# ScalarE's functions regrouped by activation table in a Mamba and mixture-of-experts kernel

## The reference, cut to what matters

```python
xn = layernorm(x)
x = x + filter_block(xn) + moe_by_sequence(xn)   # L0
xn = layernorm(x)
x = x + causal_attention(xn) + moe_by_token(xn)  # L1, 16 heads; 2 of 8 experts per token

# filter_block (L0_attn), cut:
u    = silu(conv(u_in) + conv_b)                 # 256 channels, 4 taps
dt, B, C = split(u @ x_proj)
delta = softplus(dt @ dt_proj + dt_b)
h[t] = exp(delta[t]*A) * h[t-1] + delta[t]*B[t]*u[t]   # 16 states, a scan over t
m    = ((h . C) + u*D_skip) * silu(res) @ out_proj
h    = layernorm(m + x)
q = gelu(l2norm(h @ q_w + q_b));  k = l2norm(h @ k_w + k_b)
qw = q . w_g;  G = (l2norm_over_tokens(qw) * q).sum(tokens)
hs = (G * k) @ proj + proj_b
hs = (hs * layernorm(h)) @ fl + fl_b
h2 = layernorm(hs + h)
out = layernorm(gelu(h2 @ d1 + d1_b) @ d2 + d2_b + h2)

# moe_by_sequence (L0_ffn): softmax router on the mean of the sequence, its best 2 of 8
# experts (gelu between two matmuls), weighted sum, + x, layernorm
```

## Time and profile before

| | us |
|---|---|
| median of 3 runs | 2735.15 |
| lowest, highest | 2718.67, 2745.57 |
| the profiled execution, its own time | 2738.27 |
| its span | 2736.5 |

### The profile page before, as it was taken

One profiled execution on the slowest core, in us unless ns is written; L12 is line 12 of the kernel. 1 busy time (PEld: TensorE's weight loads), 2 busy tenths in 40 slices (PEclk: granted clock), 3 DMA queues, 4 the chain that ended last, 5 costly groups with the idle time before them and its releaser, 6 DMA issues.

```text
span 2736.5 us, 38788 instructions
## 1 busy us (share of the span) xinstructions
PE 2185.6 (80%) x11640; PEld 1519.0 (56%) x11640; DVE 1644.7 (60%) x2929; ACT 1177.2 (43%) x2702; POOL 936.8 (34%) x581
## 2 busy tenths in 40 slices
PE   4257888888888788888889788987889788888885
PEld 1033566655665556655566556655666555665664
DVE  2965775557754776547764587546765477644322
ACT  2223454345533455345543465333553345423541
POOL 0421562028410473006620185103740067202501
PEclk8568889888999889989899898898899988999997
DMA  2000011311222111321113112221113211131123
GB/s 94 0 16 0 32 50 62 113 51 46 68 82 75 53 41 58 106 76 41 51 64 104 61 46 70 70 88 50 44 59 97 85 37 56 59 126 58 62 93 115
DMA packets 82452, 175.06 MB, mean 64 GB/s; under 512 B 11448, under 2 KB 42560, under 8 KB 81984
## 3 DMA queue, kind: packets, MB, share of 16 engines
q1 hardware_dynamic: 78144, 164.05, 17.9%
q0 software_dynamic: 4096, 8.40, 1.1%
HBM read 123.71 MB, written 15.14 MB: 51 GB/s over the span
## 4 chain that ended last, share of the span: by engine, by line
PE 49%; issue 17%; DVE 15%; POOL 9%; ACT 7%; DMA 1%; SPq 0%; DVEq 0%; POOLq 0%; ACTq 0%
PE G L910 8%; PE G L1032 6%; DVE HS L1509 3%; PE G L1017 3%; POOL Y L1925 3%; PE G L921 2%; PE FM L1006 2%; POOL REG L1936 2%; PE G L1049 2%; PE FM L731 2%; POOL YG L1950 2%; DVE maxes L1803 2%; PE G L1006 2%; POOL REG L1939 2%; PE FM L880 2%
## 5 line engine op out<-in xcount | busy, mean ns | idle before, releaser
L1032 PEld LDWEIGHTS G<-REG 128*128 128x128 f32 x2560 | 376.8, 213 | 79.2 <-issue 53.6
L1032 PE MATMUL G<-REG 128*128 128x64 f32 x2560 | 383.7, 286 | 18.9 <-DVE REG L1815 18.9
L1312 ACT ACTIVATE REG<-G 128x128 f32<-128x128 f32 (+3 forms) x512 | 224.1, 438 | 374.9 <-PE G L1017 371.5
L1509 DVE TENSOR_TENSOR_SCAN HS<-DA,D 128x1024 f32<-128x1024 f32 x128 | 361.8, 2827 | 31.3 <-ACT DA L1191 30.7
L1925 POOL TENSOR_TENSOR Y<-Y,HC 128x1024 f32<-128x1024 f32 x114 | 274.8, 2410 | 258.0 <-DVE HC L1531 257.4
L910 PEld LDWEIGHTS G<-XGT,MW 128*128 128x128 f32 x1920 | 294.9, 238 | 58.1 <-issue 58.1
L910 PE MATMUL G<-XGT,MW 128*128 128x128 f32 x1920 | 301.9, 324 | 19.5 <-DMA MW<-moe 19.5
L1936 POOL TENSOR_TENSOR REG<-REG,cos_t 128x512 f32<-128x512 f32 x128 | 170.4, 1331 | 341.8 <-ACT REG L1288 340.7
L1017 PE MATMUL G<-ident,REG 128*128 128x128 f32 x1280 | 248.1, 295 | 31.0 <-ACT REG L1312 29.4
L1006 PE MATMUL G<-REG 64*128 64x128 f32 (+3 forms) x768 | 233.4, 517 | 12.1 <-ACT REG L1288 6.1
L1261 ACT ACTIVATE SL<-G 128x512 f32<-128x512 f32 x120 | 71.6, 597 | 375.9 <-PE G L910 375.9
(11 more groups left out here) (284 smaller groups left out, 3972.0 us busy)
## 6 DMA issues: line engine op xcount, KB each, us to landing
MW<-moe SPq DMA_DIRECT2D x120, 768.0 KB, 4.3
REG<-ROT SPq DMA_DIRECT2D x256, 128.0 KB
EW<-experts SPq DMA_DIRECT2D x16, 514.5 KB, 4.2
XG<-x_rows SPq DMA_DIRECT2D x8, 960.0 KB, 5.6
y_rows<-YO SPq DMA_DIRECT2D x120, 64.0 KB, 1.5
X<-xT SPq DMA_DIRECT2D x8, 256.0 KB, 5.7
W<-weights SPq DMA_DIRECT2D x1, 2048.0 KB, 9.4
REG<-xT SPq DMA_DIRECT2D x8, 256.0 KB, 2.8
```

The costliest lines, as they stand in the source:

```text
L1032: mm = pe.matmul(G[3][:, col:col + DK], PT[:, n % 2, c * P:(c + 1) * P], V[:, c, j * P + h * DK:j * P + (h + 1) * DK], start=c == 0, stop= ...
L1312: act.activation(PT[:, n % 2, 0:width], G[2][:, 0:width], ACT.Copy).then_inc(pt_copy.sem, 1)
L1509: dve.tensor_tensor_scan(HS[:, :, :].rearrange("p h s -> p (h s)"), DA[:, n % 2, :, :].rearrange("p h s -> p (h s)"), D1[:, :, :].rearrang ...
```

## The change

The table of the front pieces, the places of the early states and the order of the bank users are changed, and a few operations move with them.

- The convolution u1 with its Silu goes from behind f6 to behind f3; r0 and r1 from behind f7 and f8 to behind f4; bc and dt from behind f10 and f11 to behind f6 and f7; the two dp halves from behind f15 and f16 to behind f10 and f11.
- The Exp of the softplus and its three DVE operations are a piece of their own, now x11, behind f21; Ln and DELTA are x12, behind f22. Before, they stood behind f16 and f18.
- The early scan states stand one filter step later each.
- The router's second exponential stands beside its first in f2, and DVE's five operations between them with it, ahead of the affine of H.

```diff
-        X_AFTER = {0: 1, 1: 2, 2: 3, 6: 4, 7: 5, 8: 6, 10: 7, 11: 8, 15: 9, 16: 10, 18: 11}
+        X_AFTER = {0: (1,), 1: (2,), 2: (3,), 3: (4,), 4: (5, 6), 6: (7,), 7: (8,), 10: (9,), 11: (10,), 21: (11,), 22: (12,)}
...
-        EARLY_AT = {23: ((0, 0),), 24: ((0, 1),), 25: ((0, 2), (1, 0)), 26: ((1, 1),), 27: ((1, 2),)}
+        EARLY_AT = {24: ((0, 0),), 25: ((0, 1),), 26: ((0, 2), (1, 0)), 27: ((1, 1),), 28: ((1, 2),)}
...
-                ("mean_i", "b", FM, (ni.s_centred, 1)), ("ss", "b", FM, (qk_root, 2)),
+                ("k", "b", FB, (kp_d, 1)), ("mean_i", "b", FM, (ni.s_centred, 1)), ("u1", "f", FM, (u_silu, 2)),
+                ("ss", "b", FM, (qk_root, 2)), ("r0", "f", FM, (r_silu, 1)), ("r1", "f", FM, (r_silu, 2)),
                 ("spread_q", "b", FC, (qn_d, 1)), ("spread_k", "b", FB, (kn_d, 1)), ("spread_i", "b", FM, (lni_d, 1)),
...
@@ ScalarE, front_start
                     act.activation(D1[:, h, :], F_BANK[f"dp{h}"][:, :], ACT.Abs, bias=vec("dt_b", h)).then_inc(soft.sem, 1)
-                    if h == 1:
-                        act.wait_ge(soft.sem, soft.at(f, 2))
-                        act.activation(D1[:, :, :], D1[:, :, :], ACT.Exp, scale=-1.0).then_inc(soft.sem, 1)
                 elif p == 11:
+                    act.wait_ge(soft.sem, soft.at(f, 2))
+                    act.activation(D1[:, :, :], D1[:, :, :], ACT.Exp, scale=-1.0).then_inc(soft.sem, 1)
+                elif p == 12:
                     act.wait_ge(wide_d.sem, wide_d.at(f, 2))
                     act.activation(DELTA[:, :, :], DELTA[:, :, :], ACT.Ln).then_inc(soft.sem, 1)
...
@@ ScalarE, filter_step, p == 2
                     act.activation(small[0:1, 16:24], small[0:1, 8:16], ACT.Exp, bias=small[0:1, 5:6], accum_out=small[0:1, 6:7]).then_inc(rt_act.sem, 1)
-                elif p == 4:
                     act.wait_ge(rt_d.sem, rt_d.at(b, 8))
...
@@ DVE, front_start
                     softplus_relu(f, p - 9)
-                    if p == 10:
-                        softplus(f)
-                        softplus_sum(f)
                 elif p == 11:
+                    softplus(f)
+                    softplus_sum(f)
+                elif p == 12:
                     softplus_end(f)
```

More of the change, by code:

```diff
@@ L1122, in front @@
             def front(b):
-                for p in range(12):
+                for p in range(13):
                     front_start(b, p, None)
@@ L1584, in filter_step @@
                     dve.tensor_scalar(small[0:1, 7:8], small[0:1, 24:25], -1.0, None, ALU.mult).then_inc(rt_d.sem, 1)
+                    affine(n0, b, H, vec("ln0_g"), vec("ln0_b"), h_d)
+                elif p == 3:
+                    dve.wait_ge(qsq_d.sem, qsq_d.at(b))
+                    dve.tensor_scalar(QP, F_BANK["q"][:, :], vec("q_b"), None, ALU.add).then_inc(qp_d.sem, 1)
+                    dve.wait_ge(ksq_d.sem, ksq_d.at(b))
+                    dve.tensor_scalar(KP, F_BANK["k"][:, :], vec("k_b"), None, ALU.add).then_inc(kp_d.sem, 1)
+                    centre(ni, b)
+                    dve.wait_ge(rt_act.sem, rt_act.at(b, 2))
+                    dve.reciprocal(small[0:1, 37:38], small[0:1, 36:37]).then_inc(rt_d.sem, 1)
+                    dve.wait_ge(rt_d.sem, rt_d.at(b, 9))
+                    dve.tensor_scalar(small[0:1, 40:42], small[0:1, 38:40], small[0:1, 37:38], None, ALU.mult).then_inc(rt_d.sem, 1)
                 elif p == 4:
```

47 lines of the change are left out of this document (15 added, 32 removed).

## The result

The changed kernel took 2754.18 us (median of 15 runs, 2742.19 to 2768.4); the kernel before, beside it, 2733.05 us (15 runs, 2710.35 to 2746.7). The ratio is 1.0095, with a 95% interval of 1.007 to 1.0121. The profiled execution of the changed kernel took 2746.79 us, its span was 2744.9 us.

The account below looks back on a forecast made before the run. TensorE, busy 80% of the span, was taken as the bound, so only work it waits for counts. Per lap −12.1 + 5.5 − 1.5 + 0 = −8.1 us, six times, plus 2 in the first lap: 2690 us, range 2655 to 2730.

Parts of the forecast that it names:

- first counterweight: Term B's new waits in the q/k sums, set against the gain: +5.5 us per lap.
- term C: Rest of the q/k block and norm_1: pieces leaving against the split's new wait, −1.5 us per lap, ends −4 and +1.5.
- term D: End of phase 1: late softplus and DELTA delays given back by shifted early states, 0 per lap, ends −1 and +3.
- Lap 0: First lap: no token tiles to cover new waits, a shorter chain to gain from; +2 us, ends −8 and +5.
- phase 2: The attention phase of a lap: predicted unchanged, its order kept but for one DVE operation at its start.
- Loads: ScalarE's function-table loads: 42 instead of 77, 45 us of ScalarE time, given no term of their own.
- rival of the loads: Every removed load on the path, with ScalarE's emptying as costly again: 35 × 2.6, about 2645 us; chance 0.08.
- Term A: norm_2's mean to the expert's fifth matmul: front work leaves, −12.1 us per lap, between −10 and −12.1.
- Term B: The q/k sums: new waits for Silus through a shared bank, +5.5 us per lap, ends +3.7 and +10.
- slower rival: q/k block at 1.2 GHz costs more than the expert gains: about 2758 us, deciding beyond 13.6 us per lap; chance 0.12.

Follow-up runs that it names:

- e1: The kernel before with only softplus, early states and the router's exponentials moved as in the change, the front's order left as before: 2695.48 us, ratio 0.9838.
- e8: e1 with the filter's three late Silus (u1, r0, r1) also early, as in the changed kernel: 2747.55 us, ratio 1.0052 to the kernel before.
- e4: The changed kernel with unread matmuls filling TensorE's waits in norm_1, norm_2, norm_f and norm_n: 2742.25 us, ratio 1.0009 to the kernel before.
- e9: e1 with only DELTA's sum moved, behind norm_f's centring: 2677.18 us, ratio 0.981; repeated, 2678.38 us, ratio 0.9763.
- e13: e9 with the early states' two products moved behind norm_n's statistics, still ahead of XN2: 2668.36 us, ratio 0.9755 to the kernel before.
- e14: The changed kernel with the moves of e9 and e13 at the end of phase 1: 2719.93 us, ratio 0.9939 to the kernel before.
- e10: e8 with unread matmuls filling TensorE's waits in norm_1 alone: 2752.12 us, ratio 1.005 to the kernel before.

## Why the prediction was wrong

The mechanism of the gain and the size of its first counterweight were right. Two steps failed: TensorE's clock behind the emptied waits was put at nothing in term C, and the shift of the early states was taken to give all of term D back. Lap 0, the last lap and phase 2 add to the miss.

- **Loads** are 42, as read off ScalarE's list, and no run shows a gain from their number: e1 drops 21 and wins 42 us, e8 drops 14 more and loses 52. A load takes 1283 ns, and a function whose operand is there starts some 11 ns later, in the changed kernel too. The rival of the loads is refuted. The Trainium skill ("ScalarE: Activation LUTs", What ACT_TABLE_LOAD costs) counts a drain of 1380 ns beside it, which these traces don't show.
- **Term A** was right: -10.7 us against -12.1 with -10 as the other end. Three of six laps have the 15.67 us of the lap without a front; in the others the rest is time at 1.2 GHz, in the lap shown a tile (3.36 us at 1180.46, 1.95 elsewhere) behind norm_2's variance.
- **Term B** was right: +5.5 in the lap shown, +5.9 in the mean, because one lap before had only 8.99. The 1.4 us that u1's matmuls were to win back are there: the sums behind them take 1.95 and 1.03 us, where they took 2.59 and 1.85. So the slower rival, whose price of 2758 us comes nearest to the measured time, has the wrong mechanism: bank FM's six users do not run at 1.2 GHz (the block's clock rose from 0.72 to 0.90; of its matmuls the tile between is slow, 3.36 us, as before), and B is far from its 13.6.
- **Term C** failed: -1.5 forecast, +1.2 measured. Its five pieces came about as forecast. In the lap shown, against the same lap before: spread to proj -1.5 (u1: -1.5 forecast), proj to fl +3.4 (the split: +3.3), fl to norm_1's mean -0.9 (r1: -0.9), mean to variance +0.3 (not forecast), variance to spread -0.6 (bc: -0.8), spread to the first dense matmul -1.6 (the affine: -1.6). Lap 1, all at full speed, has 40.71 us against the usual 41.97: -1.3. The step that failed is that the term ends there. It counts the matmuls behind these waits at full speed, though u1 and r1, which had filled them, are gone. From the first dense matmul to norm_2's mean the shown lap takes 15.0 us instead of 12.3, and in three other laps the stretch from norm_1's variance to its spread is 3.2 us and that of the dense layers 1.5 us longer than in lap 1. Against each kernel's lap at full speed that is 3.4 us a lap in the mean, where the kernel before loses 0.9. e8 shows such a loss from the Silus' move alone, and e4, in which C is at a clock of 1.00 throughout, shows that filling the waits removes it, at the price of the filling.
- **Term D** failed: 0 forecast, +3.3 measured. Both delays were as forecast in kind: norm_f's mean comes 1.1 us later behind the expert's sum (2.9 forecast; a token tile covers the rest), and its centring starts 2.8 us behind that mean instead of 1.3. What failed is the give-back, which was to return all of it. From the centring to X the shift of the early states returned 0.6 us, and a variance at 1.2 GHz (1.84 us instead of 1.27) took as much. Behind X the changed kernel loses another 1.1 us, between norm_n's statistics and XN2, since the shift brings GpSimd's add beside the inverse root; no row of before could show that price. e9 shows the centring's part: it starts 1.25 us behind the mean again. e13 shows that the add's part can't be had by moving one operation out of its way ahead of XN2: the next one pays.
- **Lap 0** is 6.5 and 8.0 us longer in the two executions, where I had +2 with +5 as an end. It pays B (+5.6), C (+3.6) and D (+4.1) and gains only 5.2 in A. The last lap's 2.7 us are clock: e14, with the same instructions in it, takes 113.6 us there.
- **Phase 2** was to be unchanged. Its order is, but for the one VectorE operation at its start, its length is not: in laps 1 to 6 it lies between 168.6 and 183.6 us, by its stretches at 1.2 GHz. The spread of the kernel's own runs, 27 us, was there to be read, and I forecast as if phase 2 were a constant. The medians are 21 us apart, and the longer phases 1 make up 8 of them in the second execution; whether and why the changed kernel has the longer patterns more often stays open. e10 shows only that an edit of phase 1 can come with another one.

The misses of the steady laps, +0.4 (B), +2.7 (C), +1.4 (A) and +3.3 (D), sum to 7.8 us, of a forecast gain of 8.1. From the profiled execution before to the second one of the changed kernel, -47 us were forecast and +20 measured. Of these 67 us, 46 are the six steady phases 1, 6 are lap 0's, 3 the last lap's and 12 the phases 2.

## What to carry to other kernels

Ask of each moved instruction not only what waits for it at its new place, but what will stand in the wait that it leaves: independent matmuls taken out of a chain's waits gained here what their length said (1.5 and 0.9 us) and lost more than that to 1.2 GHz behind the emptied waits (3.4 us a lap). Price such a move once at each clock. A late cluster of vector work must be laid operation by operation into the gaps of the chain it lands in (here one 1.22 us sum behind the centring instead of ahead of it was worth 0.3 to 0.8%). And an edit of several parts should be timed in parts: here half of it alone gave 1.6%, with one operation moved 1.9 to 2.4%, while the whole lost 1%. Each part's price holds beside the others only: the early front cost 1.1, 1.8 and 2.6% in three surroundings.
